# Node one-hots as the stationary operand, and a contiguous x for W2, in a message-passing layer

## The reference

```python
row, col = src, dst
h = concat([x[row], edge_attr], axis=1)          # 53125 x (128 + 64)
h = relu(batchnorm(h @ W1 + b1, g1, be1))        # over all edges
agg = segment_sum(h, col) / max(count(col), 1)   # mean per destination node
h2 = relu(batchnorm(concat([x, agg], axis=1) @ W2 + b2, g2, be2))
out = layernorm(x + relu(h2 @ Wl + bl))
```

## Time and profile before

| | |
|---|---|
| median of 3 runs | 611.88 us (611.45 to 613.88) |
| profiled execution, its own time | 613.19 us |
| its span | 611.4 us |
| PE busy | 523.2 us (86%) |
| PE loads of weights | 402.0 us (66%) |
| DVE busy | 453.0 us (74%) |
| ACT busy | 212.9 us (35%) |
| POOL busy | 387.9 us (63%) |
| gathers from the table (L685) | 352 |
| node matmuls (L788) | 1575 in 222.5 us |

### The profile page before, as it was taken

How to read it: one execution, slowest core, us unless ns; L and a number is a source line. 1 busy time by engine, 2 the same in 40 slices (tenths; PEclk the granted TensorE clock), 3 DMA queues, 4 the chain that set the end, 5 groups by cost and what they waited for, 6 DMA issues and landing times.

```text
span 611.4 us, 11185 instructions
## 1 busy us (share of the span) xinstructions
PE 523.2 (86%) x3396; PEld 402.0 (66%) x3396; DVE 453.0 (74%) x747; ACT 212.9 (35%) x568; POOL 387.9 (63%) x487
## 2 busy tenths in 40 slices
PE   4639999999999999999897989854448999999983
PEld 4527666766757677777666676632225999999573
DVE  4598878686888868797877788654435877777786
ACT  2253222232313232222222221221116456666466
POOL 4777777777777777777777777777773233333500
PEclk9778999999999999999999999975568899999998
DMA  7635434443435444444444243442232478777004
GB/s 193 229 112 172 144 119 145 149 152 106 152 125 153 147 142 133 134 130 134 130 129 139 86 140 107 126 129 94 86 103 87 131 229 229 232 233 220 13 1 105
DMA packets 49561, 84.38 MB, mean 138 GB/s; under 512 B 11490, under 2 KB 25682, under 8 KB 49521
## 3 DMA queue, kind: packets, MB, share of 16 engines
q1 hardware_dynamic: 31420, 49.21, 25.3%
q0 software_dynamic: 11648, 23.88, 15.0%
q10 hardware_dynamic: 6453, 10.79, 5.1%
HBM read 63.74 MB, written 20.08 MB: 137 GB/s over the span
## 4 chain that ended last, share of the span: by engine, by line
POOL 41%; PE 27%; issue 17%; DVE 8%; DMA 4%; ACT 2%; ACTq 0%; POOLq 0%; DVEq 0%
POOL res L685 29%; POOL work L685 11%; PE psH L929 8%; PE psC L929 8%; PE psH L788 5%; DMA res<-ytab,srci 1%; PE psT L849 1%; DVE res L1481 1%; POOL res L667 1%; DMA srci<-in_src 1%; PE psH L769 1%; DMA res<-in_x,srci 1%; DVE res L1312 1%; ACT res L1068 1%; PE psT L769 1%
## 5 line engine op out<-in xcount | busy, mean ns | idle before, releaser
L685 POOL DMA_INDIRECT res<-ytab,srci x248 | 237.3, 957 | 75.6 <-issue 73.1
L788 PE MATMUL psH<-res 125*128 125x256 bf16 (+1 forms) x1575 | 222.5, 298 | 9.6 <-DVE res L1298 8.6
L788 PEld LDWEIGHTS psH<-res 125*128 125x128 bf16 x1575 | 152.3, 98 | 72.9 <-DVE res L1298 13.4
L685 POOL DMA_INDIRECT work<-ytab,srci x104 | 98.3, 946 | 31.7 <-issue 31.4
L1312 DVE TENSOR_TENSOR res<-agg,psC 125x1280 bf16<-125x1280 bf16 (+1 forms) x105 | 99.1, 971 | 4.9 <-PE psH L788 4.8
L1298 DVE TENSOR_TENSOR res<-psH,res 128x512 f32<-128x512 f32 x50 | 34.5, 689 | 80.3 <-DMA res<-ytab,srci 42.1
L1449 DVE TENSOR_TENSOR work<-res,psX 128x512 f32<-128x512 f32 x103 | 69.7, 687 | 21.0 <-PE psC L929 15.8
L710 POOL TENSOR_TENSOR agg<-agg,srci 128x64 f32 x104 | 32.3, 311 | 72.0 <-ACT srci L1163 58.5
L1345 DVE TENSOR_TENSOR psX<-agg,psX 128x512 f32<-128x512 f32 x103 | 71.1, 690 | 2.5 <-ACT agg L1023 2.4
L769 PE MATMUL psH<-w1e,work 128*128 128x256 f32 x200 | 55.6, 403 | 11.7 <-DVE res L1298 11.7
L1023 ACT ACTIVATE agg<-res 128x512 f32<-128x512 f32 x78 | 48.7, 624 | 46.7 <-DVE res L1298 28.8
(11 more groups left out here) (204 smaller groups left out, 549.8 us busy)
## 6 DMA issues: line engine op xcount, KB each, us to landing
work<-in_edge_attr SPq DMA_DIRECT2D x26, 512.0 KB, 3.6
spill<-work SPq DMA_DIRECT2D x26, 256.0 KB, 2.4
res<-spill SPq DMA_DIRECT2D x25, 256.0 KB, 3.2
res<-ytab,srci POOLq DMA_INDIRECT x248, 2.5
hot_dram<-hotb ACTq DMA_DIRECT2D x13, 256.0 KB
hot_dram<-work ACTq DMA_DIRECT2D x13, 256.0 KB
hotb<-hot_dram SPq DMA_DIRECT2D x13, 256.0 KB, 2.7
work<-hot_dram SPq DMA_DIRECT2D x13, 256.0 KB, 2.9
```

The source lines that it names most:

```text
L685: pool.indirect_dma_start(rows[:, j * F:(j + 1) * F], None, ytab, bass.IndirectOffsetOnAxis(ap=srci[:, j, g:g + 1], axis=0)).then_inc(gath ...
L788: last = pe.matmul(noderows[:, 0:w], exact[k][0:PN, t * F:(t + 1) * F], hots[:, (t - t0) * w:(t - t0 + 1) * w], start=(t == 0 and k == 0), ...
```

## The change

Four things change.

1. Node product: the one-hots of one tile (125 nodes by 128 edges) are stationary, and the three parts of the table's block stream onto the edge product of q = 2 directly (`start=False`). The turned rows, ACT's copy and the way back go. There are three matmuls of 128 columns for each tile and block, 75 per tile.
2. `node_tiles`: three tiles in cycles 2 to 22, but two in cycles 2, 5, 8, 11 and 14.
3. x comes a second time in node order (`x_columns`); SP loads chunks of 500 nodes (`xchunk`, 250 KB) that the x product reads contiguously.
4. The order on PE and DVE is changed.

```diff
 def node_tiles(i):
-    return 2 + i % 2 if ROWS0 <= i < ROWS1 else 0
+    if not ROWS0 <= i < ROWS1:
+        return 0
+    return 2 if i < 15 and i % 3 == 2 else 3
...
-        PRODUCTS = [(0, q) for q in range(U)] + [(1, 0)]
-        for i in range(1, NI):
-            order = [(i, 1), (i, 2), (i, 3)] + ([(i + 1, 0)] if i + 1 < NI else [])
-            PRODUCTS += order if i not in NODES else order[1:] + order[:1]
+        PRODUCTS = [(0, q) for q in range(U)] + [(i, q) for i in range(1, NI) for q in range(U)]
...  SP
+            def load_x_chunk(m):
+                k, n = XCHUNKS[m]
+                if m == 0:
+                    sp.wait_ge(prod_ready, EARLY)
+                else:
+                    sp.wait_ge(x_ps, H2 * m)
+                sp.dma_start(xchunk[:, 0:n * NT], xcols[:, k * NT:(k + n) * NT]).then_inc(x_chunk, 16)
             load_ea(1, 1)
             load_nodes_of(ROWS0)
+            load_x_chunk(0)
             load_ea(2, 0)
             for i in range(NI - 3):
                 spill_out(i, i % 2)
                 load_ea(i + 3, (i + 1) % 2)
                 if i + 3 in NODES:
                     load_nodes_of(i + 3)
+                if i % 2 and i // 2 + 1 < len(XCHUNKS):
+                    load_x_chunk(i // 2 + 1)
...  PE, node_batch
-                if b == 0:
-                    pe.wait_ge(h_ready, U * (i - 1) + 2)
                 pe.wait_ge(nhot_ready, batch_index(i, b) + 1)
                 hots = node_chunks(i, b)
                 for t in range(t0, t1):
-                    for k in range(PARTS):
-                        last = pe.matmul(noderows[:, 0:w], exact[k][0:PN, t * F:(t + 1) * F],
-                                         hots[:, (t - t0) * w:(t - t0 + 1) * w], start=(t == 0 and k == 0),
-                                         stop=(t == NT - 1 and k == PARTS - 1))
+                    for j in range(node_tiles(i)):
+                        at = (t - t0) * w + j * P
+                        for k in range(PARTS):
+                            last = pe.matmul(psP[NODEQ][:, j * F:(j + 1) * F], hots[:, at:at + P],
+                                             exact[k][0:PN, t * F:(t + 1) * F], start=False,
+                                             stop=(t == NT - 1 and j == node_tiles(i) - 1 and k == PARTS - 1))
...  PE: rows_back is gone; x_product reads xchunk
                 pe.wait_ge(cnt_placed, m + 1)
-                pe.matmul(psT[1][:, 0:n * NT].rearrange("o (p t) -> o p t", t=NT), w2x[:, h * P:(h + 1) * P],
-                          xtv[:, :, k:k + n].rearrange("f t p -> f p t"), start=True, stop=True).then_inc(x_ps, 1)
+                pe.wait_ge(x_chunk, 16 * (m // H2 + 1))
+                pe.matmul(psT[1][:, 0:n * NT], w2x[:, h * P:(h + 1) * P], xchunk[:, 0:n * NT], start=True, stop=True
+                          ).then_inc(x_ps, 1)
...  PE, edge_step
                 node = i in NODES
+                product(i, par, nth, 2)
                 if node:
                     node_batch(i, 0)
                     node_batch(i, 1)
-                else:
-                    product(i, par, nth, 1)
                 if i <= len(XSTEPS):
                     x_product(i - 1)
-                product(i, par, nth, 2)
+                product(i, par, nth, 3)
                 if node:
                     node_batch(i, 2)
-                product(i, par, nth, 3)
-                if node:
                     node_batch(i, 3)
-                    node_batch(i, 4)
                 if i + 1 < NI:
                     product(i + 1, 1 - par, (i + 1) // 2 + 1, 0)
+                if node:
+                    node_batch(i, 4)
                 counts(i, par)
-                if node:
-                    pe.wait_ge(rows_kept, i - ROWS0 + 1)
-                    product(i, par, nth, 1)
-                    rows_back(i)
+                if i + 1 < NI:
+                    product(i + 1, 1 - par, (i + 1) // 2 + 1, 1)
...  ACT: rows_out is gone
             for i in range(1, NI - 1):
-                if i in NODES:
-                    rows_out(i)
                 squares(i, 0)
...  DVE, make_h: h(i, 2) waits for the last batch; edge_step
-                    dve.wait_ge(rows_added, i - ROWS0 + 1)
+                    dve.wait_ge(nhot_used, NB5 * (i - ROWS0 + 1))
...
                     if q == 0:
+                        node_onehots(i, 4)
+                        onehots(i + 1)
+                    if q == 1:
                         node_onehots(i + 1, 0)
                         node_onehots(i + 1, 1)
-                    if q == 1:
-                        onehots(i + 1)
-                        node_onehots(i + 1, 2)
-                    if q == 2:
-                        node_onehots(i + 1, 3)
-                        node_onehots(i + 1, 4)
+                    if q >= 2:
+                        node_onehots(i + 1, q)
```

More of the change, by code:

```diff
@@ L55, in node_tiles, with gnn_kernel @@
 def node_tiles(i):
-    return 2 + i % 2 if ROWS0 <= i < ROWS1 else 0
-def gnn_kernel(nc, E, x, xt, src, src_rows, dst, dst_rows, ea, W1, b1, g1, be1, W2, b2, g2, be2, Wl, bl, out):
+    if not ROWS0 <= i < ROWS1:
+        return 0
+    return 2 if i < 15 and i % 3 == 2 else 3
+def gnn_kernel(nc, E, x, xt, xcols, src, src_rows, dst, dst_rows, ea, W1, b1, g1, be1, W2, b2, g2, be2, Wl, bl, out):
     N, F = x.shape
@@ L126, in gnn_kernel @@
         nodeid = sb("nodeid", [P, NT])[:, :]
-        rowst_sb = sb("node_rows_turned", [P, MOST * P])
         nodepair = sb("node_pairs", [P, 2 * NT], BF16)
@@ L214, in gnn_kernel @@
         XSTEPS = [(h, k, min(XP, PN - k)) for k in range(0, PN, XP) for h in range(H2)]
+        XCHUNKS = [(k, n) for h, k, n in XSTEPS if h == 0]
         w2x = agg[:, 0:H2 * P]
@@ L223, in gnn_kernel @@
         assert SQ0 >= NAGG // 2 and SQ0 + 2 * GF <= NAGG - MOST * P
-        assert XW <= 512 and len(XSTEPS) <= XT0 // (KEEP * GF) - 1
+        xchunk = agg[:, SQ0 - GF:SQ0 - GF + XW]
+        assert Z0 + MOST * P <= SQ0 - GF
+        assert XW <= 512
         psT = [pb(f"psT{i}", [P, 512]) for i in range(2)]
@@ L234, in gnn_kernel @@
         gram = psT[0][:, F:2 * F]
-        noderows = psP[1][:, 0:MOST * P]
         iotap = psC[0][:, 0:WIN]
@@ L278, in gnn_kernel @@
         nhot_used = sem("node_onehots_used")
-        rows_kept = sem("node_rows_turned_copied")
-        rows_added = sem("node_rows_added")
         s_cols = sem("cols_loaded")
@@ L293, in gnn_kernel @@
         s_tab = sem("table_written")
+        x_chunk = sem("x_chunk_loaded")
         x_ps = sem("w2_x_psum")
@@ L678, in gather @@
                     pool.wait_ge(spilled[i % 2], 16 * (i // 2))
-                if (i + 1) * KEEP * GF > XT0 and q == 0:
-                    pool.wait_ge(x_ps, len(XSTEPS))
                 if (i + 1) * KEEP * GF > TAB0 and q == 0:
@@ L786, in node_batch @@
                 for t in range(t0, t1):
-                    for k in range(PARTS):
-                        last = pe.matmul(noderows[:, 0:w], exact[k][0:PN, t * F:(t + 1) * F],
-                                         hots[:, (t - t0) * w:(t - t0 + 1) * w], start=(t == 0 and k == 0),
-                                         stop=(t == NT - 1 and k == PARTS - 1))
-                last.then_inc(nhot_used, 1)
-            def rows_back(i):
-                pe.wait_ge(rows_kept, i - ROWS0 + 1)
[L796 to L799, removed]
+                    for j in range(node_tiles(i)):
[4 more added lines that the diff above has]
+                                             stop=(t == NT - 1 and j == node_tiles(i) - 1 and k == PARTS - 1))
+                last.then_inc(nhot_used, 1)
             def ea_cols(par, q, b):
@@ L882, in _ @@
             product(1, 1, 1, 0)
+            product(1, 1, 1, 1)
             for i in range(1, NI):
@@ L1611 @@
         'x_turned': x.reshape(N // NT, NT, F).transpose(2, 1, 0),
+        'x_columns': x.T,
         'src': src.reshape(NG, P, TILES).transpose(1, 2, 0),
```

## The result

The changed kernel takes 641.09 us (median of 4 runs, 639.70 to 642.90), the kernel before, beside it, 612.75 us. The ratio is 1.0465, 95% interval 1.0428 to 1.0502. Slower was forecast, with 626 us: of the 28.3 us lost, the forecast had half, 12.1 by its sum for the profiled execution and 14.1 by 626 against the median of 611.88.

The account below looks back on a forecast made before the run. POOL's gathers, one every 1.25 us, bound the kernel, PE close behind. Afterwards a closed loop makes h(14, 2) 24 us late; after absorption the last gather is 12.1 us later: 613.19 + 12.1 = 625.3, stated as 626 us, range 613 to 652.

Parts of the forecast that it names:

- The closed loop: Cycles 2 to 14: h(i, 2) to h(i+1, 2) through PE, ACT, DVE; mean 18.9 us against POOL's 16.7.
- The x product's saving: On PE: contiguous instead of strided reading of x saves 1.0 us in each of 12 cycles.
- the loads on SP: Seven more loads, for the chunks of x, counted at zero; 7 us if each held the next edge load.
- the sum's last one: End of the edge phase: from gather (22, 3), 51 intervals of 1.25 us, 63.8 us, last gather at 477.6.
- the price of the matmuls on the loop: On PE: 90 node matmuls of batches 0 and 1 at 55.9 ns each, 5.03 us per three-tile cycle.
- A: Edge phase: POOL keeps the pace and six fewer gathers make the kernel faster, 605.7 us; chance 0.10.
- B: Node products on PE: loads cost something, 60 to 68 ns per matmul, 636 to 657 us; chance 0.17.
- C: Node products on PE: loads not hidden, 70 to 98 ns per matmul, 686 us at 77 ns; chance 0.08.
- D: Cycles 2 to 14: excess over POOL's pace half of that counted, time about the same, 609 to 615 us; chance 0.05.

Follow-up runs that it names:

- e4: The changed kernel with 36 or 18 idle bf16 matmuls on PE, filling most of its wait for h(i, 2) in cycles 2 to 13: 635.62 us.
- e1: The changed kernel with ACT's copy of the x product moved behind squares(i, 2) and (i, 3): 608.9 us, ratio 0.9952.
- e2: The changed kernel with the x product on PE moved ahead of node batches 0 and 1: 608.6 us, ratio 0.9945.
- e6: The changed kernel with the x product read with a stride again and without the chunk loads: 651.11 us, ratio 1.0633.
- e8: The kernel before with only the contiguous x product and its chunk loads added: 611.01 us, ratio 0.9974.
- e5: The changed kernel with the x product first on PE, its copy last on ACT, and two node tiles in cycle 22: 604.63 us, ratio 0.9876.
- e7: The changed kernel with the tile counts of before, two in even cycles and three in odd ones: 630.38 us, ratio 1.0283.
- e9: The changed kernel with no node tiles in cycle 22 and idle matmuls in PE's wait for h(i, 2): 630.77 us, ratio 1.0277.
- e3: The changed kernel with no node tiles in cycle 22, which gathers all 16 tiles: 637.35 us, ratio 1.0414.

## Why the prediction had the direction right and the size wrong

*What held.* The closed loop is there, through the engines and instructions that the prediction names; the chain of cycle 4 shows 19.18 us for 19.2, e4 has 20.0, 19.2, 17.7 in turn, and e1 and e2 open it at two different places. A node matmul takes 55.9 ns. From cycle 16 on a cycle takes 16.6 us for 16.5. The x product's saving was right (e6), and the loads on SP, counted at nothing, show no loss (e8).

*What failed, first step:* the sum's last one: "From there 4 + 48 = 52 gathers, 51 x 1.25 = 63.8: the last starts at 477.6". Between gather (22, 3) and the last there is a wait that I left out, though it is a line of `gather` (L682, kept from the kernel before): gather (23, 0) waits for the last node batch of cycle 22. It cost 7.5 us (the 7.76 of the row, less the 0.3 of issue). The prediction's own times hold it: the last batch of cycle 22 ends right before h(22, 2), at 409.9 + 16.5 = 426.4, and gather (23, 0) was due at 413.8 + 5.0 = 418.8, 7.6 us earlier. The loop isn't its cause, for e1 and e2 have it too with the loop open (5.5 and 6.9 us); cycle 22 now has three tiles for PE and one gather fewer for POOL, and with two again it is gone (e5, e7). I had read the diff for moved waits and not asked what else waits for the moved instructions.

*Second step:* the price of the matmuls on the loop, taken at the full clock (1.00, the 2.4 GHz level) for all cycles. The prediction's own sums left PE idle for 3 us a cycle (15.9 us of work in 18.9), and in the kernel before the clock stood at 1.00 with PE busy for 159.1 of 162 us. It didn't ask whether the clock would stay with PE's new gaps. Cycles 3, 6, 9, 12 and 15 cost 2.4 + 1.6 + 1.6 + 1.5 + 1.6 = 8.7 us more. Of these the 2.4 us of cycle 3 aren't the loop's alone: the lower clock is there in e1, e2 and e5 too, with the loop open, behind the late rows.

The account of the last gather, 477.6 forecast and 495.74 measured:

| from | us |
|---|---|
| h(2, 2) at 69.7 instead of 69.0 (late rows from the gather) | +0.7 |
| lower clock in cycles 3, 6, 9, 12, 15 | +8.7 |
| the other cycles up to 21 | +0.4 |
| from h(21, 2) (419.7 for 409.9) to POOL's last gather of cycle 22 | +0.9 |
| wait of gather (23, 0) | +7.5 |
| sum (18.1 by the two times; the rest is rounding) | +18.2 |

The first row is what is left of two: h(1, 2) started at 49.39 us, 2.0 earlier than the 51.41 that the prediction took from the kernel before, and cycle 2 took 20.4 us instead of 17.6.

In times: 625.3 forecast for the profiled execution and 642.9 measured is 17.6; the rest after the last gather was 0.4 us shorter. With both missed terms taken away (e9), the last gather is at 484.36. The forecast's 477.6 with three gathers more (3.75) would be 481.4; the 3.0 us left are 2.5 us at h(21, 2), 1.6 of them in cycle 15, where e9's clock fell (e4's didn't) and which takes 18.1 us, and 0.5 after it.

*The rivals.* A fell for this order (POOL waits 37.5 us for h by the two rows above), and e5 shows it was only a matter of the order and of cycle 22. B and C fell: the spacing is 55.9 ns, over 90 matmuls in a row, and 4350 of them were run. The Trainium skill (TensorE: Matmul & The Clock Gate, section Back-to-back issue gap) gives 81 ns for a stream of load-matmul pairs with 128 columns; no stretch at the full clock bears that out here, and the measurement decides. The formula of the same section of the Trainium skill for an isolated matmul (columns divided by 2.4 GHz, plus 2.5 ns: about 56 ns) is what the stream shows. D fell with the account above. The range (613 to 652) held by luck: its upper part was made from dearer loads, and what filled it were the wait and the clock.

## What to carry to other kernels

Where engines run in written order, draw the closed loops that a reordering makes and add them up; PE's 84% busy said nothing here, and one copy moved on another engine (e1) was worth some 31 us. For each moved instruction, look up every wait on the semaphores that it raises, in unchanged code too, above all where one buffer follows another in the same memory. And where a forecast puts gaps on PE, price the matmuls behind them at both clock levels.

## What the runs showed of the hardware

- Bf16 matmuls of 128 columns, each with its own load of 128 columns, follow at 55.9 ns (90 in 5.03 us), though the record of each load is 99 ns and of each matmul 219 ns. Before, a matmul of 256 columns took 109.3 ns: two or three times as many loads per column cost nothing that the spacing shows, but 2.5 ns for each matmul more.
- In cycles 6, 9, 12 and 15 a wait of PE of 2.69 us was followed by some 3.4 us at the 1.2 GHz level, in PE's first work after the wait, and this took 1.5 to 1.6 us a time. In cycle 3, behind waits of 2.31 and 2.98 us, it was 6.8 us at that level and 2.4 us lost. 18 or 36 matmuls without use in the gap (e4) went with 1.00 from 50 to 410 us and made the kernel 5.5 us faster.
- The same wait did not always bring it: 2.88 us in e3 left the clock at 1.00, so did 2.69 us in e7's cycles 7 and 11 and before e4's cycle 15. What tells them apart stays open.
